# Three early tiles with additions on GpSimd, and the fourth quad's rows prepared sooner, in an embedding and CIN kernel

## The chip, the core and the metric

The kernel runs on one core of one Trainium2 chip. The metric is the device time of one execution, in microseconds. Three runs of the kernel before took 682.30, 683.49 and 684.36 us; their median is 683.49 us. The profiled execution took 684.21 us, and the span that its trace covers is 682.3 us.

## What is computed

512 samples have 39 features each. Every feature is looked up in its own table (16 floats a row), and three CIN layers of 128 maps, then a small MLP, follow:

```python
e = jnp.stack([tbl_0[ids[:, 0]], ..., tbl_38[ids[:, 38]]], axis=1)      # 512 x 39 x 16
def _cin_layer(X0, Xi, W, b):
    Wr = W.reshape(H, F0_, Fi)
    return jnp.einsum('hjk,bjd,bkd->bhd', Wr, X0, Xi) + b[None, :, None]
Xi = X0
for W, b in Ws:                     # three layers
    Xi = _cin_layer(X0, Xi, W, b)
    res.append(Xi.sum(axis=2))
h = jnp.concatenate([z, dense_ctx], axis=1)
h = jnp.maximum(h @ W_top1 + b_top1, 0.0)
h = jnp.maximum(h @ W_top2 + b_top2, 0.0)
y = h @ W_top3
```

Only the sum over the 16 positions of layers 2 and 3 is wanted, which the kernel uses.

## The kernel before

**Tiles and quads.** A tile is 8 samples by 16 positions, 128 partitions. There are 64 tiles, T = 0 to 63; four of them make a quad, q = 0 to 15. Tile T belongs to quad T // 4, and ti = T % 4 is its place there.

**A tile's work (layer 1 of the code).** TensorE makes ten groups of up to four features, g = 0 to 9 (group 8 has three). Each group is three matmuls (L995, L996, L997: a product of split numbers) into one of five PSUM banks, bank g % 5. Group g can begin only when the bank's last reader is through with group g - 5, or with group g + 5 of the tile before (L987). Groups 2, 5 and 8 are read by VectorE, which scales and adds up in `scale_and_sum` (L802); the other seven are read by ScalarE, which scales them into `prod` (`scale`, L611). So group 3 of a tile waits for VectorE's group 8 of the tile before. `y_made` counts the groups that TensorE has finished: 10 T + g + 1 behind group g of tile T.

**The reductions.** `reduce_early(T)` on VectorE (L809) sums what ScalarE's first five groups (0, 1, 3, 4, 6) left in `prod`, and stands on VectorE's queue between its groups 5 and 8. `reduce_late(T)` (L817) sums the rest and stands ahead of the next tile's group 2. From quad 2 on (FREE_QUADS = 2), GpSimd first adds four of the ten pairs of `prod` onto others, in two additions of a tile (`add_groups`, L428; the first waits for ScalarE's group 1, the second for its group 4), and the early reduction is over six pairs; it waits for GpSimd then. In tiles 0 to 7 GpSimd makes no additions, and the early reduction is over all ten. ScalarE's first group of the next tile waits for the early reduction (`scale`, L608).

**A quad's rows.** What layer 0 of quad q needs runs through every engine, ahead of its use:
1. GpSimd makes the indices and issues ten gathers, 0 to 9 (`gather`, L399). Those of quads 2 to 4 are gated by `GATHERED_AT`, a count of y_made for each.
2. SyncE waits for all ten to land and copies the rows to `emb_room` in 16 DMAs (`lay_out`, L297).
3. GpSimd repeats them in `emb_room` when these have landed (`repeat_rows`, L411 and L413).
4. TensorE turns them into `ps_tr` (`turn_rows`, L879), and ScalarE keeps the result as x0 (`keep_x0`, L535). For quads 1 and 2 this is done at the places in NEXT_TURNED_AFTER and NEXT_KEPT_AFTER, for quad 3 (during quad 1) at THIRD_TURNED_AFTER = (3, 1) and THIRD_KEPT_AFTER = (3, 3), which are a ti and a group of quad 1, and for later ones at TURNED_AFTER and KEPT_AFTER.
5. SyncE shares x0 out (`share_rows`, three DMAs, L305) and cuts six windows (`cut_window`, L310), and then lays out the next quad's rows.
6. GpSimd multiplies seven chunks (`multiply`, L423). Chunk 0 waits for the shared rows, chunk 1 for all six windows.
7. TensorE sums the seven chunks (`layer0`, L910), between the groups of the quad before. ScalarE and VectorE split the result (`keep_x1`, L546; `split_x1`, L727; `sum_x1`, L732).

**Order.** Every engine runs its own queue in the order written. GpSimd's for quads 0 and 1 is written out by hand (L466 to L500), and the loop over tiles with `between` (L502 to L520) begins with tile 8. TensorE's other work (`sum_d`, L1012, behind group 6; `turn_x`, L887; `turn_w2`, L900) stands between groups too.

Of the kernel before, what the change touches and what calls it, by code (L numbers as in the profile page):

```python
# [8 lines left out]
AX_XY = mybir.AxisListType.XY  # L9
# [11 lines left out]
QT = 4  # L21
# [9 lines left out]
GATHERS = -(-F // FPG)  # L31
# [23 lines left out]
ADDED = [(0, 1), (2, 3)]  # L55
EARLY = slice(4, 10)
EARLY_FIRST = slice(0, 10)
LATE = [slice(10, 16), slice(11, 17)]
ACCS = [10, 16]
BIASED = 15  # L60
# [12 lines left out]
REPEATED_IN = (1, 1)  # L73
TURNED_AFTER, KEPT_AFTER = (2, 4), (2, 6)
FREE_QUADS = 2
THIRD_TURNED_AFTER, THIRD_KEPT_AFTER = (3, 1), (3, 3)
SUMMED_AFTER = {(0, 2): 0, (0, 5): 1, (0, 8): 2, (1, 1): 3, (1, 8): 4, (2, 8): 5, (3, 2): 6}
THIRD_SUMMED_AFTER = {(0, 4): 0, (0, 7): 1, (0, 9): 2, (1, 2): 3, (1, 8): 4, (2, 8): 5, (3, 2): 6}
SECOND_SUMMED_AFTER = {(1, 9): 0, (2, 1): 1, (2, 3): 2, (2, 5): 3, (2, 7): 4, (3, 0): 5, (3, 2): 6}
# [3 lines left out]
SECOND_REGROUPED_AFTER = 3  # L83
NEXT_TURNED_AFTER, NEXT_KEPT_AFTER = [(0, 7), (0, 1)], [(0, 7), (0, 3)]

GATHERED_AT = {2: [0, 8, 9, 11, 13, 15, 17], 3: [0, 0, 0, 0, 42, 44, 46, 48, 50, 52],
               4: [54, 56, 58, 66, 68, 72, 73, 75, 76, 78]}
SUM_D_AFTER = 6

# [26 lines left out]
def wait(engine, semaphore, value):  # L116
    if value > 0:
        engine.wait_ge(semaphore, value)


def gather_rows(g):
# [3 lines left out]
def laid_through(q):  # L125

    return 16 * FPG * DG * (q - 1)


def chunk_rows(c):  # L130
    return F * sum(c + CHUNKS * a < SHIFTS for a in range(SPC))


def build(nc, dense_ctx, ids, bases, table, W_top1, b_top1, W_top2, b_top2, W_top3, W0, b0, W1, b1, W2, b2, out):
# [8 lines left out]
    with ExitStack() as ctx:  # L143
        def sb(name, shape, dt=F32):
            return ctx.enter_context(nc.sbuf_tensor(name, shape, dt))

        def sem(name):
            return ctx.enter_context(nc.semaphore(name))
# [40 lines left out]
        prod = sb("prod", [P, PAIRS, H, 2])  # L189
# [66 lines left out]
        dve_step, act_step, pool_step = sem("dve_step"), sem("act_step"), sem("pool_step")  # L256
# [32 lines left out]
        def _(sp):  # L289
            def lay_out(q):  # L290
                wait(sp, gathered[q % 2], 16 * GATHERS * (q // 2 + 1))
                wait(sp, emb_turned, q)
                for f in range(FPG):
                    n = len(range(f, F, FPG))
                    src = rows[QB * f:QB * (f + 1), q % 2, 0:n, :]
                    for e in range(DG):
                        sp.dma_start(packed[QB * e:QB * (e + 1), f:F:FPG, :],  # L297
                                     src[:, :, DI * e:DI * (e + 1)]).then_inc(laid_out, 16)

            def share_rows(q, landed):  # L300

                wait(sp, z_made, CHUNKS * q)
                for a in range(SPC):
                    at = -CHUNKS * a % F
                    sp.dma_start(xa[F * a:F * (a + 1), :], x0[at:at + F, q % 2, :]).then_inc(landed, 16)  # L305
# [77 lines left out]
        def _(pool):  # L383
            def make_index(q):

                wait(pool, laid_out, laid_through(q - 2) if q > 3 else 0)
                if q == 2:
                    pool.wait_ge(regrouped_dve, 1)
                    pool.wait_ge(regrouped_act, 1)
                if q == 3:  # L390
                    pool.wait_ge(regrouped_pool, 1)
                    pool.wait_ge(regrouped_act, 2)
                nc.gpsimd.tensor_tensor(index[:, q % 2, :], ids_all[:, q * GATHERS:(q + 1) * GATHERS], base[:],
                                        ALU.add).then_inc(index_made, 1)
                wait(pool, index_made, q + 1)

            def gather(q, g):
                n = gather_rows(g)
                pool.indirect_dma_start(  # L399
                    out=rows[0:n, q % 2, g, :], out_offset=None, in_=table,  # L400
                    in_offset=bass.IndirectOffsetOnAxis(ap=index[0:n, q % 2, g:g + 1], axis=0),
                ).then_inc(gathered[q % 2], 16)

            def repeat_rows(q):
                if q == 1:
                    pool.wait_ge(regrouped_pool, 1)
                    pool.wait_ge(regrouped_act, 2)
                else:
                    pool.wait_ge(laid_out, laid_through(q))
                n, last = F * DI, (XROWS - REP) * DI  # L410
                nc.gpsimd.tensor_copy(emb_room[:, n:SPC * n].rearrange("p (r n) -> p r n", n=n),  # L411
                                      emb_room[:, None, 0:n].broadcast_to([P, SPC - 1, n]))
                nc.gpsimd.tensor_copy(emb_room[:, SPC * n:SPC * n + last], emb_room[:, 0:last]).then_inc(emb_made, 1)  # L413

            def multiply(q, c):
                if c == 0:
                    wait(pool, shared[q % 2], 16 * SPC * ((q + 1) // 2))
                    wait(pool, z_used, CHUNKS * (q - 1) + 1)
                if c == 1:
                    wait(pool, cut[q % 2], 16 * (CHUNKS - 1) * ((q + 1) // 2))  # L420
                r = chunk_rows(c)
                window = bz[0:r, c, :] if c else x0[0:r, q % 2, :]
                nc.gpsimd.tensor_tensor(bz[0:r, c, :], window, xa[0:r, :], ALU.mult).then_inc(z_made, 1)  # L423
# [43 lines left out]
            def gather_behind(q, g):  # L467
                wait(pool, y_made, GATHERED_AT[q][g])
                gather(q, g)

            for g in range(len(GATHERED_AT[2])):
                gather_behind(2, g)
            for c in range(CHUNKS):
                multiply(1, c)
                if len(GATHERED_AT[2]) + c < GATHERS:
                    gather(2, len(GATHERED_AT[2]) + c)
            make_index(3)
            for g in range(4):
                gather_behind(3, g)
            repeat_rows(2)  # L480
            for g in range(4, 8):
                gather_behind(3, g)
            multiply(2, 0)
            for g in range(8, GATHERS):
                gather_behind(3, g)
            multiply(2, 1)
            multiply(2, 2)
            make_index(4)
            for g in range(3):
                gather_behind(4, g)  # L490
                multiply(2, 3 + g)
            multiply(2, 6)
            for g in range(3, 5):
                gather_behind(4, g)
            repeat_rows(3)
            for g in range(5, 9):
                gather_behind(4, g)
            multiply(3, 0)
            gather_behind(4, 9)
            multiply(3, 1)  # L500
# [169 lines left out]
        def _(dve):  # L670
# [82 lines left out]
            n, last = F * DI, (XROWS - REP) * DI  # L753
# [50 lines left out]

            def reduce_early(T):
                dve.wait_ge(act_step, ACT_STEPS * T + 5)
                wait(dve, pool_step, len(ADDED) * (T + 1 - FREE_QUADS * QT))
                wait(dve, reduced, REDUCTIONS * T)
                nc.vector.tensor_reduce(prod[:, BIASED, :, 0], prod[:, EARLY if T >= FREE_QUADS * QT else EARLY_FIRST].rearrange("p n h l -> p h n l"), AX_XY,  # L809
                                        ALU.add).then_inc(reduced, 1)  # L810

            def reduce_late(T):
# [11 lines left out]
            for T in range(TILES):  # L824
# [16 lines left out]
                if ti == 3 and FREE_QUADS <= q < QUADS - 1:  # L841
                    split_x1(q + 1)
                    sum_x1(q + 1)
                reduce_early(T)
                if T == 0:
                    split_rest_x1()
# [6 lines left out]
                if T in W2_TURNED_IN:  # L853
                    n = W2_TURNED_IN[T]
# [256 lines left out]
```

## Time and profile before

| | before |
|---|---|
| median of three runs | 683.49 us |
| profiled execution | 684.21 us |
| its span | 682.3 us |
| TensorE (PE) | 664.0 us busy, 97% |
| ScalarE (ACT) | 567.3 us busy, 83% |
| VectorE (DVE) | 512.4 us busy, 75% |
| GpSimd (POOL) | 443.4 us busy, 65% |

The profile is one execution taken by the hardware's profiler. "Busy" is the time in which an engine had at least one instruction under way. Matmuls are pipelined, so two records next to each other overlap by some 0.16 us, and the idle time in a row is a little less than what was lost. In a timeline a row is a start, a length, the engine, the line of the kernel, the operation with what it writes and reads, how many instructions were merged, and in brackets the idle time ahead of it with the engine and line that ended it. The releaser is inferred, and where a DMA or another wait came last it can name the wrong one.

### The profile page before, as it was taken

The numbers are of one execution on the slowest core, as the hardware profiler recorded it, in microseconds if no ns is written. First come the engines' busy times: TensorE is split into PE (matmuls) and PEld (weight loads), VectorE is DVE, ScalarE is ACT, GpSimd is POOL, SyncE is SP. The second block draws the span as 40 slices with busy tenths as digits, with TensorE's granted clock in tenths as the row PEclk, the third lists the DMA queues.
The fourth block names the chain that finished last, engine by engine and source line by source line (L and its number), as shares of the span: only waits on it lengthen the run. The fifth ranks groups of instructions, "written<-read, shape, count | busy, mean of one in ns | idle before, by whom it ended". The sixth has DMA issues, their size and how long they took to land.

```text
span 682.3 us, 10404 instructions
## 1 busy us (share of the span) xinstructions
PE 664.0 (97%) x2702; PEld 491.7 (72%) x2702; DVE 512.4 (75%) x984; ACT 567.3 (83%) x1997; POOL 443.4 (65%) x437
## 2 busy tenths in 40 slices
PE   4899999999999999999999999999999999999998
PEld 4766776677777777777777777777777777776683
DVE  5687887687787778777877787787878777888680
ACT  3586978798888888898988889888989898998672
POOL 6658374887778877788787777887788556333000
PEclk9899999999999999999999999999999999999899
DMA  6231234232423333333312212131313141005200
GB/s 211 77 96 9 56 58 120 38 98 11 153 40 110 85 94 99 68 98 68 97 8 77 29 38 65 13 90 5 98 7 98 5 139 37 0 1 184 116 1 1
DMA packets 107533, 46.04 MB, mean 67 GB/s; under 512 B 80897, under 2 KB 92941, under 8 KB 107474
## 3 DMA queue, kind: packets, MB, share of 16 engines
q1 hardware_dynamic: 101427, 42.82, 23.8%
q0 software_dynamic: 5120, 1.29, 2.2%
q10 hardware_dynamic: 927, 1.26, 0.7%
q8 instruction: 22, 0.36, 0.2%
q14 instruction: 37, 0.30, 0.1%
HBM read 13.81 MB, written 5.24 MB: 28 GB/s over the span
## 4 chain that ended last, share of the span: by engine, by line
PE 83%; ACT 1%; issue 1%; POOL 1%; DVE 0%; DMA 0%; SPq 0%; ACTq 0%; DVEq 0%; POOLq 0%
PE ps_y L995 19%; PE ps_y L997 18%; PE ps_y L996 18%; PE ps_x L910 12%; PE ps_g L1012 4%; PE ps_tr L879 1%; PE ps_y L1058 1%; PE ps_y L1056 1%; PE ps_y L1057 1%; ACT prod L611 1%; PE ps_y L1070 1%; PE ps_y L1006 1%; PE ps_tr L887 1%; PE ps_tr L900 1%; POOL room L423 1%
## 5 line engine op out<-in xcount | busy, mean ns | idle before, releaser
L611 ACT ACTIVATE prod<-ps_y,xt 128x128 f32<-128x128 f32 x1792 | 493.9, 431 | 75.2 <-PE ps_y L997 67.4
L995 PE MATMUL ps_y<-w_hi,x_hi 128*128 128x512 f32 (+1 forms) x640 | 312.8, 489 | 5.2 <-DVE prod L802 2.5
L996 PE MATMUL ps_y<-w_lo,x_hi 128*128 128x512 f32 (+1 forms) x640 | 249.6, 390 | 0.0
L997 PE MATMUL ps_y<-w_hi,x_lo 128*128 128x512 f32 (+1 forms) x640 | 249.5, 390 | 0.0
L428 POOL TENSOR_TENSOR prod<-prod 128x512 f32<-128x512 f32 x112 | 144.5, 1291 | 99.5 <-ACT prod L611 97.5
L802 DVE SCALAR_TENSOR_TENSOR prod<-ps_y,xt,prod 128x128 f32<-128x128 f32 x576 | 165.0, 344 | 45.1 <-PE ps_y L997 44.7
L399 POOL DMA_INDIRECT rows<-in_table,index x160 | 154.1, 963 | 49.6 <-issue 26.5
L809 DVE TENSOR_REDUCE prod<-prod 128x128 f32<-128x1536 f32 (+1 forms) x64 | 120.6, 1884 | 65.7 <-ACT prod L611 65.7
L995 PEld LDWEIGHTS ps_y<-w_hi,x_hi 128*128 128x128 f32 x640 | 120.8, 189 | 58.6 <-issue 24.6
L996 PEld LDWEIGHTS ps_y<-w_lo,x_hi 128*128 128x128 f32 x640 | 121.0, 189 | 48.5 <-issue 25.0
L423 POOL TENSOR_TENSOR room<-room 117x512 f32<-117x512 f32 (+1 forms) x105 | 135.2, 1290 | 24.2 <-DMA room<-room 21.4
L997 PEld LDWEIGHTS ps_y<-w_hi,x_lo 128*128 128x128 f32 x640 | 120.8, 189 | 25.9
L817 DVE TENSOR_REDUCE x<-prod 128x128 f32<-128x1536 f32 x64 | 112.0, 1750 | 13.2 <-ACT prod L611 10.9
L910 PE MATMUL ps_x<-room,w0t 117*128 117x512 f32 (+1 forms) x210 | 108.0, 595 | 1.5 <-POOL room L423 1.4
L910 PEld LDWEIGHTS ps_x<-room,w0t 117*128 117x128 f32 (+1 forms) x210 | 38.6, 189 | 9.3 <-POOL room L423 3.3
L1012 PE MATMUL ps_g<-bd,x 128*128 128x320 f32 x128 | 44.8, 431 | 0.0
L800 DVE TENSOR_SCALAR prod<-ps_y,xt 128x128 f32<-128x128 f32 x128 | 38.6, 344 | 0.4 <-PE ps_y L997 0.4
L620 ACT COPY g_all<-ps_g 128x320 f32<-128x320 f32 x64 | 31.2, 488 | 3.4 <-PE ps_g L1012 3.4
L655 ACT CAST g_hi<-g_all 128x512 fp32r<-128x512 f32 x39 | 23.9, 621 | 6.2 <-PE ps_y L1058 4.0
L1012 PEld LDWEIGHTS ps_g<-bd,x 128*128 128x128 f32 x128 | 24.0, 188 | 6.1 <-DVE x L817 0.5
L720 DVE TENSOR_TENSOR bd<-ps_tr,mask 128x1248 f32<-128x1248 f32 x16 | 23.2, 1448 | 0.0
L869 DVE TENSOR_TENSOR x_hi<-g_all,g_hi 128x512 fp32r<-128x512 f32 x20 | 13.8, 691 | 5.5 <-ACT g_hi L655 5.5
(120 smaller groups left out, 329.1 us busy)
## 6 DMA issues: line engine op xcount, KB each, us to landing
room<-room SPq DMA_DIRECT2D x75, 234.0 KB
room<-room SPq DMA_DIRECT2D x45, 78.0 KB
emb_room<-rows SPq DMA_DIRECT2D x168, 5.0 KB
rows<-in_table,index POOLq DMA_INDIRECT x160
w_hi_dram<-g_all SPq DMA_DIRECT2D x5, 512.0 KB, 4.3
w_lo_dram<-g_all SPq DMA_DIRECT2D x5, 512.0 KB, 5.1
room<-room SPq DMA_DIRECT2D x15, 156.0 KB
g_all<-in_L_rec_W SPq DMA_DIRECT2D x9, 256.0 KB, 6.0
```

Source lines behind the costliest of these rows:

```text
L399: pool.indirect_dma_start(out=rows[0:n, q % 2, g, :], out_offset=None, in_=table, in_offset=bass.IndirectOffsetOnAxis(ap=index[0:n, q % 2, ...
L423: nc.gpsimd.tensor_tensor(bz[0:r, c, :], window, xa[0:r, :], ALU.mult).then_inc(z_made, 1)
L428: nc.gpsimd.tensor_tensor(prod[:, SLOT[a]:SLOT[a] + 2], prod[:, SLOT[a]:SLOT[a] + 2], prod[:, SLOT[b]:SLOT[b] + 2], ALU.add).then_inc(pool ...
L611: ins = nc.scalar.activation(prod[:, SLOT[k] + m // 2, :, m % 2], ps_y[:, g % YBANKS, m * H:(m + 1) * H], ACT.Copy, scale=xt[:, q % 2, ti, ...
L802: ins = nc.vector.scalar_tensor_tensor(out=a, in0=y, scalar=x, in1=a, op0=ALU.mult, op1=ALU.add)
L809: nc.vector.tensor_reduce(prod[:, BIASED, :, 0], prod[:, EARLY if T >= FREE_QUADS * QT else EARLY_FIRST].rearrange("p n h l -> p h n l"), ...
L817: nc.vector.tensor_reduce(x2[:, T % 2, :], prod[:, LATE[T % 2]].rearrange("p n h l -> p h n l"), AX_XY, ALU.add).then_inc(reduced, 1)
L910: nc.tensor.matmul(ps_x1[:], w0t[0:r, c, :], bz[0:r, c, :], start=c == 0, stop=c == CHUNKS - 1).then_inc(z_used, 1)
L995: nc.tensor.matmul(y, hi, w1_hi[:, cols], start=True, stop=False)
L996: nc.tensor.matmul(y, hi, w1_lo[:, cols], start=False, stop=False)
L997: nc.tensor.matmul(y, lo, w1_hi[:, cols], start=False, stop=True).then_inc(y_made, 1)
L1012: nc.tensor.matmul(ps_g[:, 0:(F + 1) * TB], x2[:, T % 2, :], bd[:, T // QT % 2, T % QT].rearrange("p j b -> p (j b)"), start=True, stop=Tr ...
```

## The change

It touches tiles 0 to 7 only.

- GpSimd makes its two additions in tiles 3, 4 and 7 too, and VectorE's early reduction of these is over six pairs. The new function `adds(T)` tells which tiles have them, and the reduction's count of GpSimd's steps is made with it.
- The gates of quad 3's last six gathers go down by four groups each.
- On GpSimd's queue, the additions stand: tile 3's behind gather 3 of quad 3 and ahead of repeat_rows(2); tile 4's around gather 7 of quad 3; tile 7's around gather 7 of quad 4. Gather 8 of quad 3 moves ahead of multiply(2, 0), and repeat_rows(3) moves from behind gather 4 of quad 4 to behind multiply(2, 6), ahead of gather 3.
- TensorE turns quad 3's rows behind group 9 of tile 6 instead of behind group 1 of tile 7, and ScalarE keeps them behind its group 0 of tile 7 instead of its group 3.

```diff
-THIRD_TURNED_AFTER, THIRD_KEPT_AFTER = (3, 1), (3, 3)
+
+ADDED_EARLY = [3, 4, 7]
+THIRD_TURNED_AFTER, THIRD_KEPT_AFTER = (2, 9), (3, 0)
...
-GATHERED_AT = {2: [0, 8, 9, 11, 13, 15, 17], 3: [0, 0, 0, 0, 42, 44, 46, 48, 50, 52],
+GATHERED_AT = {2: [0, 8, 9, 11, 13, 15, 17], 3: [0, 0, 0, 0, 38, 40, 42, 44, 46, 48],
...
+def adds(T):
+    return T >= FREE_QUADS * QT or T in ADDED_EARLY
...
             make_index(3)
             for g in range(4):
                 gather_behind(3, g)
+            add_groups(3, 0)
+            add_groups(3, 1)
             repeat_rows(2)
-            for g in range(4, 8):
+            for g in range(4, 7):
                 gather_behind(3, g)
+            add_groups(4, 0)
+            gather_behind(3, 7)
+            add_groups(4, 1)
+            gather_behind(3, 8)
             multiply(2, 0)
-            for g in range(8, GATHERS):
-                gather_behind(3, g)
+            gather_behind(3, 9)
             multiply(2, 1)
             multiply(2, 2)
             make_index(4)
@@
                 gather_behind(4, g)
                 multiply(2, 3 + g)
             multiply(2, 6)
+            repeat_rows(3)
             for g in range(3, 5):
                 gather_behind(4, g)
-            repeat_rows(3)
-            for g in range(5, 9):
+            for g in range(5, 7):
                 gather_behind(4, g)
+            add_groups(7, 0)
+            gather_behind(4, 7)
+            add_groups(7, 1)
+            gather_behind(4, 8)
             multiply(3, 0)
             gather_behind(4, 9)
             multiply(3, 1)
...
             def reduce_early(T):
                 dve.wait_ge(act_step, ACT_STEPS * T + 5)
-                wait(dve, pool_step, len(ADDED) * (T + 1 - FREE_QUADS * QT))
+                if adds(T):
+                    dve.wait_ge(pool_step, len(ADDED) * sum(adds(t) for t in range(T + 1)))
                 wait(dve, reduced, REDUCTIONS * T)
-                nc.vector.tensor_reduce(prod[:, BIASED, :, 0], prod[:, EARLY if T >= FREE_QUADS * QT else EARLY_FIRST].rearrange("p n h l -> p h n l"), AX_XY,
+                nc.vector.tensor_reduce(prod[:, BIASED, :, 0], prod[:, EARLY if adds(T) else EARLY_FIRST].rearrange("p n h l -> p h n l"), AX_XY,
                                         ALU.add).then_inc(reduced, 1)
```

## Rows read from the trace of the kernel before

**Rows 1.** The page's first line.
```profile
span 682.3 us, 10404 instructions
```

**Rows 2.** TensorE's waits between 60 and 600 us: total, times, longest.
```profile
PE ps_y L995 <- DVE prod L802: 2.5, 2, 1.4
PE ps_x L910 <- POOL room L423: 0.7, 1, 0.7
```

**Rows 3.** TensorE's timeline, 75 to 129 us: start us, us, then what ran.
```profile
75.04 0.40 PE L997 MATMUL ps_y<-w_hi,x_lo 128*128 128x512 f32 x1
75.56 0.50 PE L995 MATMUL ps_y<-w_hi,x_hi 128*128 128x512 f32 x1
...
84.31 0.50 PE L995 MATMUL ps_y<-w_hi,x_hi 128*128 128x512 f32 x1 [1.13 <-DVE prod L802]
...
101.82 0.40 PE L995 MATMUL ps_y<-w_hi,x_hi 128*128 128x512 f32 x1
...
115.33 0.50 PE L995 MATMUL ps_y<-w_hi,x_hi 128*128 128x512 f32 x1 [1.39 <-DVE prod L802]
...
121.67 1.13 PE L910 MATMUL ps_x<-room,w0t 117*128 117x512 f32 x2 [0.74 <-POOL room L423]
...
123.64 0.40 PE L997 MATMUL ps_y<-w_hi,x_lo 128*128 128x512 f32 x1
124.15 1.12 PE L910 MATMUL ps_x<-room,w0t 117*128 117x512 f32 x2
...
127.22 1.02 PE L910 MATMUL ps_x<-room,w0t 117*128 117x512 f32 x2
128.28 0.49 PE L995 MATMUL ps_y<-w_hi,x_hi 128*128 128x512 f32 x1
```

**Rows 4.** VectorE's timeline: early reductions of tiles 3, 4, 7, 8; two others.
```profile
71.91 2.82 DVE L809 TENSOR_REDUCE prod<-prod 128x128 f32<-128x2560 f32 x1 [0.28 <-ACT prod L611]
...
80.66 2.82 DVE L809 TENSOR_REDUCE prod<-prod 128x128 f32<-128x2560 f32 x1 [0.83 <-ACT prod L611]
83.40 0.86 DVE L802 SCALAR_TENSOR_TENSOR prod<-ps_y,xt,prod 128x128 f32<-128x128 f32 x3
...
111.68 2.82 DVE L809 TENSOR_REDUCE prod<-prod 128x128 f32<-128x2560 f32 x1 [0.76 <-ACT prod L611]
...
125.69 1.75 DVE L809 TENSOR_REDUCE prod<-prod 128x128 f32<-128x1536 f32 x1 [5.53 <-ACT prod L611]
...
137.41 1.74 DVE L817 TENSOR_REDUCE x<-prod 128x128 f32<-128x1536 f32 x1
```

**Rows 5.** GpSimd's timeline, 71 to 139 us.
```profile
71.01 0.44 POOL L411 COPY emb_room<-emb_room 128x312 f32<-128x312 f32 x1 [3.85 <-DMA emb_room<-rows]
...
85.60 0.92 POOL L399 DMA_INDIRECT rows<-in_table,index  x1 [0.31 <-PE ps_y L997]
89.24 2.54 POOL L423 TENSOR_TENSOR room<-room 117x512 f32<-117x512 f32 x2 [2.72 <-PE ps_y L997]
...
98.18 2.53 POOL L423 TENSOR_TENSOR room<-room 117x512 f32<-117x512 f32 x2
...
120.34 1.27 POOL L423 TENSOR_TENSOR room<-room 117x512 f32<-117x512 f32 x1 [4.20 <-DMA room<-room]
...
138.61 1.29 POOL L428 TENSOR_TENSOR prod<-prod 128x512 f32<-128x512 f32 x1 [0.91 <-ACT prod L611]
```

**Rows 6.** ScalarE's timeline: tile 4's first groups, x0 of quads 2, 3.
```profile
74.82 3.26 ACT L611 ACTIVATE prod<-ps_y,xt 128x128 f32<-128x128 f32 x12 [0.54 <-issue]
77.88 0.66 ACT L535 COPY room<-ps_tr 123x512 f32<-123x512 f32 x1
...
108.96 0.61 ACT L535 COPY room<-ps_tr 123x512 f32<-123x512 f32 x1
```

**Rows 7.** SyncE's issues of lay_out for quads 2 and 3.
```profile
58.40 11.28 SPq L297 DMA_DIRECT2D emb_room<-rows  x16
...
89.43 10.60 SPq L297 DMA_DIRECT2D emb_room<-rows  x16
```

## Prediction

> **What bounds the kernel now.** I read the page's span and its busy shares first, then TensorE's waits, then TensorE's timeline, and only then the engines it waited for. The span is 682.3 us [rows 1] and TensorE is busy for 97% of it. Between 60 and 600 us it waits three times, 3.2 us in total: twice for VectorE's L802, once for GpSimd's L423 [rows 2]. All three lie before 122 us. From there on the kernel is as long as TensorE's own stream, so what happens on another engine counts only where it reaches TensorE before about 130 us.
>
> The waits view understates the loss, since the records of pipelined matmuls overlap. A group's L997 starts 0.23 us before the next matmul starts in an undisturbed stretch, and an L910 pair 0.46 us. Whatever is more is lost. Read so, the timeline [rows 3] has six losses from tile 4 on:
> - 0.29 us before 75.56 (tile 4, group 3: 75.56 - 75.04 - 0.23)
> - 1.30 us before 84.31 (tile 5, group 3: 1.13 idle, plus the 0.17 of overlap)
> - 1.55 us before 115.33 (tile 8, group 3: 1.39 + 0.16)
> - 0.90 us before 121.67 (layer 0 of quad 3, chunk 1: 0.74 + 0.16)
> - 0.28 us before 124.15 (chunk 2: 0.51 - 0.23)
> - 0.60 us before 128.28 (tile 9, group 3: 1.06 - 0.46)
>
> They add up to 4.92 us, which is the most that this change can win.
>
> Two causes stand behind them. Group 3 of a tile needs the PSUM bank of the tile before's group 8, which VectorE reads right after the early reduction. In quads 0 and 1 that reduction is over ten pairs and takes 2.82 us; with GpSimd's additions it takes 1.75 us [rows 4]. In tile 4 it starts at 80.66, group 8 follows at 83.40 and is done at 84.26, and TensorE goes on at 84.31. In tile 7 it starts at 111.68 and TensorE goes on at 115.33. Tile 3's does the same for the 0.29. The other three losses are quad 3's rows: its multiply of chunk 1 on GpSimd stood until 120.34 for the windows [rows 5], which came 10.8 us after x0 was kept (108.96 + 0.61 = 109.57) [rows 6]. Behind that multiply tile 8's additions were queued too, so its early reduction stood 5.53 us, to 125.69 [rows 4], and tile 9 lost its 0.60.
>
> **Part 1: additions in tiles 3, 4 and 7.** Six additions of 1.29 us are added on GpSimd [rows 5], 7.7 us; three reductions lose 2.82 - 1.75 = 1.07 us each on VectorE. An addition can end no sooner than ScalarE's group 4 plus 1.3 us, while the reduction waits for ScalarE's group 6 anyway, 1.0 us behind group 4 (a group of four is 3.26/12 x 4, about 1.0) [rows 6]. So the reduction starts about 0.3 us later than with ScalarE alone.
> - Tile 3: ScalarE's group 6 released the reduction at 71.91; its group 4 ended near 70.9, so the second addition runs to 72.2, and the reduction goes from 72.25 to 74.0 instead of to 74.73. Group 8 is done about 74.8: the 0.29 is gone. ScalarE had been idle 0.54 before 74.82, released by this reduction; it now starts tile 4 at 74.1, 0.7 sooner, and keeps quad 2's x0 at 77.2 instead of 77.88 [rows 6].
> - The additions stand ahead of quad 2's repeat_rows on GpSimd's queue, which ran at 71.01 when its copies had landed [rows 5]. It now ends near 72.7 instead of 71.6. Its reader, turn_rows(2), comes after tile 4's group 1, at 73.8: 1.1 us of cover, cost nothing.
> - Tile 4: ScalarE's groups 0 and 1 end by 76.25 and group 4 (behind the x0 copy) by 78.8. GpSimd: repeat_rows to 72.7; gathers 4, 5 and 6 of quad 3 to 76.3 (1.25 each, the last gated by tile 4's group 1); first addition 76.35 to 77.6; gather 7 to 78.7; second addition 78.85 to 80.1. Reduction 80.2 to 81.95, group 8 done at 82.8. TensorE wants group 3 of tile 5 at 84.31 - 1.30 - 0.29 = 82.7. So 0.1 is left of 1.30.
> - Tile 7: TensorE is then 1.5 us sooner (less the wait of part 2). ScalarE no longer copies x0 between groups 3 and 4 (0.47). The second addition ends near 110.2, the reduction runs 110.25 to 112.0, group 8 is done at 112.8, where TensorE wants it at 112.6: 0.25 is left of 1.55.
>
> The Trainium skill speaks against this part: "Perfetto Trace Analysis", section "Optimizing Scalar/DVE Operations", says that the two engines share an SBUF port, so that moving work from one to the other might not help. In this trace it does not show: an addition from 138.61 to 139.90 lies over a reduction from 137.41 to 139.15, and both have their usual lengths, 1.29 and 1.74 [rows 4, 5].
>
> **Part 2: quad 3 sooner.** The chain has four links, and each is set by a different engine.
> - Gathers. Their gates move four groups down, but the last one (9) is also behind multiply(2, 0), which waits for quad 2's x0 to be shared out. That comes 0.7 sooner (the copy above), at 82.2. The last gather therefore starts near 83.55 instead of 85.60 [rows 5]: 2.05 us won, not four groups.
> - Copies on SyncE. lay_out(3) started at 89.43, 3.83 after the last gather's start, and took 10.60 to issue [rows 7]. The copies of quad 2 were issued by 69.68 and GpSimd went on at 71.01, so they land 1.33 later. Now: 83.55 + 3.83 = 87.4, issued by 98.0, landed by 99.35. It is not delayed by SyncE's queue, whose window cuts for quad 2 end before 85.3.
> - repeat_rows(3) now stands right behind multiply(2, 6). That one ended at 100.71, 11.47 us after the windows of quad 2 came at 89.24 [rows 5]; the windows come 0.7 sooner, so it ends at 100.0. Then 0.59 for the repeat: 100.6. So GpSimd's own queue is later than the copies, by 0.6.
> - turn_rows(3) stands at the end of tile 6, where TensorE arrives at 101.82 - 1.5 = 100.3 [rows 3]. It waits about 0.3. This is a new wait, and behind it on TensorE's queue is all of tile 7. The turn itself (0.70) is only moved.
>
> What it brings: x0(3) is kept after tile 7's group 0, near 103.7 instead of 109.57. By the 10.8 us above chunk 1 has its windows at 114.4 instead of 120.34. GpSimd meets this after gathers, additions and multiply(3, 0) at 113.7; chunk 1 is multiplied by 115.7, chunk 2 by 118.2, tile 8's second addition ends at 119.7. TensorE wants chunk 1 at 118.3 and chunk 2 at 120.5 (before's times less the losses removed), and tile 9's group 3 at 124.0, for which group 8 is ready at 122.2. So 0.90, 0.28 and 0.60 all go, with 1.8 us or more of cover each.
> Quad 4's rows: their last gather is still behind multiply(3, 0), and goes from 115.2 to 112.7; its copies land by 129, ahead of GpSimd's repeat near 130.5. Cost nothing.
>
> **The sum.** 0.29 + 1.20 - 0.30 + 1.30 + 0.90 + 0.28 + 0.60 = 4.27 us, call it 4.25. Behind 130 us there was no wait to absorb or to renew it, and the end follows TensorE one to one. Span 682.3 - 4.25 = 678.05. The profiled execution took 684.21, so it would take 679.96; the three runs have the median 683.49, 0.72 below it, which gives **679.2 us**.
>
> **Rivals.**
> - *The turn waits longer.* Were the gathers' landing tied to the windows' traffic, so that lay_out(3) went no sooner than before (issued by 100.03), the rows would land at 101.4, be repeated at 102.0, and TensorE would wait 1.7 instead of 0.3: 4.25 - 1.4 gives 680.6. For it: 3.83 us for one gather's landing is long and falls in the cuts' traffic. Against: the windows are cut sooner as well. 12%.
> - *The additions come too late.* Gathers stand ahead of them with 0.1 us to spare in tile 4. One gather's slip (1.25) puts both second additions back; 1.1 of tile 5's and 1.2 of tile 8's losses return: gain 1.9, 681.6. Against: ScalarE's group 4, and not the queue, comes last by the times above. 12%.
> - *Quad 3's rows come sooner but the losses at 121 to 128 stay*, because GpSimd is late in tile 8 with one thing or another (six extra operations, 7.7 us). Gain 4.25 - 1.78 = 2.5, 681.0. Against: 2.6 us of cover on chunk 1. 8%.
> - *Port*: reductions and additions take turns. An addition then ends up to 1.75 later, so the losses of tiles 5 and 8 return in full (2.5): 681.7. The Trainium skill's page "SBUF — State Buffer", section "SBUF: two separate sides", calls the pair an exclusive lock for some operations. The overlapping rows speak against it. 3%.
> - *Slower.* TensorE stands at turn_rows(3) for more than it wins: the gain ahead of that wait and behind it is 4.55, so it decides once the rows are repeated later than 100.3 + 4.55 = 104.9. With copies 7 us later than worked out (107) it is 2 us slower, 685.5. Against it: before, GpSimd found the rows landed by 103.1. 3%.
>
> **How the numbers follow.** The forecast has 62%; its own range is 678.2 to 680.4 (a wait of 0 to 1.2 at the turn, 0.3 either way on each reduction, and the runs' scatter). The range for 8 in 10 goes from 677.9 (all 4.92, and a median 0.7 below) to 681.9, which takes in the rivals at 680.6, 681.0 and 681.6. Within 0.3%, about what a measurement of this kernel can tell from no change, means above 681.4: half of the late additions, the port and a part of the others, 16%. Slower by more: 4%. Faster by more: 80%.
>
> **What would show it.** TensorE's waits for L802 fall from 2.5 us to about 0.2 and the one for L423 is gone; there is a short new one at L879 near 100.5. Tile 4's early reduction takes 1.75 and starts near 80.2. The last gather of quad 3 starts near 83.5, lay_out(3) at 87.4, x0(3) is kept near 103.1. A wait at L879 of over 1 us, or additions that start long after ScalarE's group 4, would prove it wrong.

## Result and the profile after

The first comparison (six runs of each) gave the changed kernel a median of 677.94 us against 683.44, a ratio of 0.9922 with the 95% interval 0.991 to 0.9934. Two later comparisons of the same kernel (e1 and e11) gave 0.9946 (0.993 to 0.9963) and 0.9953 (0.9929 to 0.9976). They are not quite of one mind: by their medians the gain is 5.5, 3.9 and 3.6 us, by their ratios 5.3, 3.7 and 3.2. In the two profiles of the first comparison 2.9 us of the difference lie outside the work that was changed, as shown below. What the change itself brings is 3.6 to 3.7 us by the traces (three of the changed kernel against one of before).

The page after, first lines (share of the span, instructions). TensorE's share is 98% instead of 97%, over a span that is 6.6 us shorter [rows 1]:

```profile
span 675.7 us, 10410 instructions
PE 659.9 (98%) x2702; PEld 489.6 (72%) x2702; DVE 509.4 (75%) x984; ACT 568.2 (84%) x1997; POOL 452.4 (67%) x443
```

Line numbers have moved: L1011 to L1013 were L995 to L997, L817 was L802, L825 was L809, L833 was L817, L434 was L428, L429 was L423, L895 was L879, L1028 was L1012, L926 was L910, L626 was L611, L417 and L419 were L411 and L413. In e2's kernel these numbers are one higher from L550 on. TensorE's waits between 60 and 600 us, where before had 3.2 us [rows 2]:

```profile
PE ps_y L1011 <- DVE prod L817: 0.5, 2, 0.3
```

And its timeline at the four places that matter [rows 3]:

```profile
81.08 0.40 PE L1013 MATMUL ps_y<-w_hi,x_lo 128*128 128x512 f32 x1
81.68 0.50 PE L1011 MATMUL ps_y<-w_hi,x_hi 128*128 128x512 f32 x1 [0.20 <-DVE prod L817]
...
98.95 0.39 PE L1013 MATMUL ps_y<-w_hi,x_lo 128*128 128x512 f32 x1
99.41 1.16 PE L895 MATMUL ps_tr<-ident,emb_room 128*123 128x128 f32 x4
100.33 0.48 PE L1011 MATMUL ps_y<-w_hi,x_hi 128*128 128x512 f32 x1
...
111.35 0.40 PE L1013 MATMUL ps_y<-w_hi,x_lo 128*128 128x512 f32 x1
112.00 0.50 PE L1011 MATMUL ps_y<-w_hi,x_hi 128*128 128x512 f32 x1 [0.26 <-DVE prod L817]
...
117.44 1.02 PE L926 MATMUL ps_x<-room,w0t 117*128 117x512 f32 x2
```

Three small losses are left: 81.68 - 81.08 - 0.23 = 0.37 us at tile 5's group 3 (1.30 before), 0.42 at tile 8's (1.55 before), and at the turn 0.23 ahead of it plus 0.22 within it (99.41 to 100.33 is 0.92, where before's turn took 0.70). The losses at chunks 1 and 2, at tile 4's group 3 and at tile 9's are gone: the pair at 117.44 follows its neighbour at once.

**A ruler for the change.** Everything that was edited lies between TensorE's sum_d in tile 2 and the one in tile 9. Before, they start at 60.00 and 131.74, 71.74 us apart. After:

```profile
58.68 0.70 PE L1028 MATMUL ps_g<-bd,x 128*128 128x320 f32 x2
...
126.69 0.70 PE L1028 MATMUL ps_g<-bd,x 128*128 128x320 f32 x2
```

That is 68.01, so the stretch is **3.73 us** shorter. By losses it is 4.92 - 0.37 - 0.45 - 0.42 = 3.68: the two ways of reading agree in sum (e4 shows that single losses are less exact). The spans differ by 6.6: 1.3 us of that had come before tile 2, and 1.6 came behind 600 us, neither place touched. The windows of both profiles show what differed there. First before, then after (busy us and instructions of each engine; the column behind POOL is TensorE's mean granted clock as a share of the full one):

```profile
28.00:32.00 4.00, 4.00 (x12) 3.00 (x11) 2.27 (x6) 2.30 (x8) 1.62 (x2) 0.62 0.55 164
620.00:640.00 20.00, 20.00 (x60) 11.03 (x59) 13.03 (x24) 12.51 (x41) 2.60 (x2) 0.91 0.69 256
```

```profile
28.00:32.00 4.00, 4.00 (x17) 2.70 (x16) 1.89 (x5) 2.82 (x11) 1.84 (x3) 1.00 0.58 173
620.00:640.00 20.00, 20.00 (x69) 11.80 (x68) 14.76 (x23) 13.60 (x31) 1.30 (x1) 1.00 0.55 212
```

Before's profiled run had two stretches of lower clock, the changed kernel's had none.

### The profile page after: what moved, and what is told of

The parts are those of the page before. It is cut to its first block, busy times and chain, and to the rows that moved or that the text cites. A ratio compares the mean times of both kernels' runs of the same rounds, so it can differ in the third digit from the quotient of the medians.

```text
span 675.7 us, 10410 instructions
## 1 busy us (share of the span) xinstructions
PE 659.9 (98%) x2702; PEld 489.6 (72%) x2702; DVE 509.4 (75%) x984; ACT 568.2 (84%) x1997; POOL 452.4 (67%) x443
## 4 chain that ended last, share of the span: by engine, by line
PE 81%; ACT 1%; issue 0%; DVE 0%; POOL 0%; DVEq 0%; ACTq 0%
PE ps_y L1011 19%; PE ps_y L1013 18%; PE ps_y L1012 18%; PE ps_x L926 12%; PE ps_g L1028 4%; PE ps_tr L895 1%; PE ps_y L1074 1%; PE ps_y L1073 1%; PE ps_y L1072 1%; ACT prod L626 1%; PE ps_y L1086 1%; PE ps_y L1022 1%; PE ps_tr L903 1%; PE ps_tr L916 1%; PE ps_tr L1022 0%
## 5 line engine op out<-in xcount | busy, mean ns | idle before, releaser
L626 ACT ACTIVATE prod<-ps_y,xt 128x128 f32<-128x128 f32 x1792 | 494.9, 433 | 69.2 <-PE ps_y L1013 63.3
L1011 PE MATMUL ps_y<-w_hi,x_hi 128*128 128x512 f32 (+1 forms) x640 | 312.5, 488 | 3.3 <-issue 1.8
L1013 PE MATMUL ps_y<-w_hi,x_lo 128*128 128x512 f32 (+1 forms) x640 | 248.9, 389 | 0.0
L1012 PE MATMUL ps_y<-w_lo,x_hi 128*128 128x512 f32 (+1 forms) x640 | 248.8, 389 | 0.0
L434 POOL TENSOR_TENSOR prod<-prod 128x512 f32<-128x512 f32 x118 | 152.4, 1291 | 104.1 <-ACT prod L626 102.2
L817 DVE SCALAR_TENSOR_TENSOR prod<-ps_y,xt,prod 128x128 f32<-128x128 f32 x576 | 165.0, 343 | 45.4 <-PE ps_y L1013 45.1
L825 DVE TENSOR_REDUCE prod<-prod 128x128 f32<-128x1536 f32 (+1 forms) x64 | 117.4, 1834 | 63.1 <-ACT prod L626 63.1
L1011 PEld LDWEIGHTS ps_y<-w_hi,x_hi 128*128 128x128 f32 x640 | 120.5, 188 | 55.5 <-issue 24.6
L1012 PEld LDWEIGHTS ps_y<-w_lo,x_hi 128*128 128x128 f32 x640 | 120.7, 189 | 48.8 <-issue 25.2
L429 POOL TENSOR_TENSOR room<-room 117x512 f32<-117x512 f32 (+1 forms) x105 | 135.4, 1292 | 17.5 <-DMA room<-room 17.3
L1013 PEld LDWEIGHTS ps_y<-w_hi,x_lo 128*128 128x128 f32 x640 | 120.4, 188 | 25.7
L833 DVE TENSOR_REDUCE x<-prod 128x128 f32<-128x1536 f32 x64 | 112.0, 1749 | 12.9 <-ACT prod L626 10.5
L926 PE MATMUL ps_x<-room,w0t 117*128 117x512 f32 (+1 forms) x210 | 107.8, 594 | 0.5 <-POOL room L429 0.5
L1028 PE MATMUL ps_g<-bd,x 128*128 128x320 f32 x128 | 44.8, 431 | 0.0
L926 PEld LDWEIGHTS ps_x<-room,w0t 117*128 117x128 f32 (+1 forms) x210 | 38.8, 189 | 7.6 <-POOL room L429 1.4
L1028 PEld LDWEIGHTS ps_g<-bd,x 128*128 128x128 f32 x128 | 24.0, 188 | 6.1 <-DVE x L833 0.5
L895 PEld LDWEIGHTS ps_tr<-ident,emb_room 128*123 128x123 f32 x64 | 15.7, 311 | 1.8 <-issue 0.7
```

The source lines that it names most:

```text
L434: nc.gpsimd.tensor_tensor(prod[:, SLOT[a]:SLOT[a] + 2], prod[:, SLOT[a]:SLOT[a] + 2], prod[:, SLOT[b]:SLOT[b] + 2], ALU.add).then_inc(pool ...
L626: ins = nc.scalar.activation(prod[:, SLOT[k] + m // 2, :, m % 2], ps_y[:, g % YBANKS, m * H:(m + 1) * H], ACT.Copy, scale=xt[:, q % 2, ti, ...
L817: ins = nc.vector.scalar_tensor_tensor(out=a, in0=y, scalar=x, in1=a, op0=ALU.mult, op1=ALU.add)
L833: nc.vector.tensor_reduce(x2[:, T % 2, :], prod[:, LATE[T % 2]].rearrange("p n h l -> p h n l"), AX_XY, ALU.add).then_inc(reduced, 1)
L926: nc.tensor.matmul(ps_x1[:], w0t[0:r, c, :], bz[0:r, c, :], start=c == 0, stop=c == CHUNKS - 1).then_inc(z_used, 1)
L1011: nc.tensor.matmul(y, hi, w1_hi[:, cols], start=True, stop=False)
```

## Experiments

In each profile I read the same ruler, sum_d of tile 2 to sum_d of tile 9: 71.74 us before, 68.01 changed.

### e1: the changed kernel again

> The changed kernel again, beside the kernel before. TensorE's losses between 60 and 130 us add up to a gain of 3.7 us (4.92 lost before, 0.37 + 0.42 + 0.45 left), but the spans of the two profiles differ by 6.6 and the medians by 5.5. Theory 1 (the rest is scatter: a granted clock below 1.00 in stretches that the change does not touch, which fell on the profile of before): over five rounds the gain is 3.7 to 4.5 us, and both kernels show runs at 1.00 and below it. Theory 2 (the change itself moves the clock): the gain stays at 5.5, and the changed kernel's mean clock is above that of before in nearly every run.

Measured: 0.9946 (0.993 to 0.9963), 3.7 us. The ruler again read 68.01, but the span was 678.9, 3.2 us more than in the same kernel's first profile, and here the low clock is back in both places:

```profile
28.00:32.00 4.00, 4.00 (x12) 3.08 (x12) 1.95 (x5) 2.30 (x8) 1.94 (x2) 0.62 0.57 169
620.00:640.00 20.00, 20.00 (x61) 11.30 (x60) 13.12 (x25) 12.23 (x33) 2.34 (x2) 0.91 0.62 242
```

So theory 1: these dips come and go with the same instructions. The runs say it too. Over the comparisons of e1 to e8, before's runs with a mean clock of 1.000 have a mean of 681.3 us (11 runs), those at 0.997 682.4 (29) and those at 0.995 684.1 (11). The changed kernel's (its first comparison and e1) have 677.6 (5), 678.3 (8) and 680.8 (3). At equal clock the difference is 3.7, 4.1 and 3.3 us, and both kernels show the same three values. The runs of before are from two chips here, so this is a rough comparison.

### e2: the additions alone

```diff
-THIRD_TURNED_AFTER, THIRD_KEPT_AFTER = (2, 9), (3, 0)
+THIRD_TURNED_AFTER, THIRD_KEPT_AFTER = (3, 1), (3, 3)
-3: [0, 0, 0, 0, 38, 40, 42, 44, 46, 48]
+3: [0, 0, 0, 0, 42, 44, 46, 48, 50, 52]
```
(against the changed kernel; repeat_rows(3) is back behind gather 4 of quad 4, tile 4's additions stand around gather 6 of quad 3, and gather 8 is back behind multiply(2, 0).)

> Only the additions in tiles 3, 4 and 7; quad 3's rows as before. Theory 1 (the losses are in series: what tile 8 wins is waited for again at quad 3's chunk 1, since x0 of quad 3 is tied to tile 7's group 3): gain 1.2 us (0.29 + 0.93), tile 8's group 3 waits 0.4 and chunk 1 of quad 3 then about 2.0 instead of 0.90. Rival (the parts add): gain 2.35 us (1.2 and 1.13 at tile 8), chunk 1 waits 0.90 as before. If the clock theory 2 holds for the change as a whole, either may be 1 to 2 us more.

Measured: 1.0001 (0.9983 to 1.0019), the ruler 71.36, a gain of 0.38. TensorE at tile 8's group 3 and at chunks 1 and 2:

```profile
112.43 0.50 PE L1012 MATMUL ps_y<-w_hi,x_hi 128*128 128x512 f32 x1 [0.72 <-DVE prod L818]
...
119.58 1.12 PE L927 MATMUL ps_x<-room,w0t 117*128 117x512 f32 x2 [1.53 <-POOL room L429]
122.05 1.13 PE L927 MATMUL ps_x<-room,w0t 117*128 117x512 f32 x2
```

Tile 8's loss fell by 0.67 (1.55 to 0.88), and chunk 1's rose by 0.80 (0.90 to 1.70): in series, as the theory had it, and the gain of tile 8 is waited away. The gain had been put at 1.2, and two sizes were off. Tile 8 lost 0.88, not 0.4: ScalarE still copied x0 between tile 7's groups 3 and 4 (see e3). At tile 5 I had reckoned with 0.37 and 1.13 was lost. Gates 44 and 46 hold gathers 5 and 6, and the additions are queued behind them: the second one ran from 78.10 to 79.39, 19.8 us after sum_d of tile 2, against 19.0 (77.72 to 79.01) in the changed kernel. e6 asks the same more sharply.

### e3: quad 3's rows alone

```diff
-ADDED_EARLY = [3, 4, 7]
+ADDED_EARLY = []
```
(with the six add_groups calls taken out of GpSimd's queue.)

> Only quad 3's rows sooner (gathers, repeat, turn and keep), no additions in quads 0 and 1. Theory: the 0.90, 0.28 and 0.60 us at 121 to 128 us go, tiles 5 and 8 keep their 1.30 and 1.55; the rows are repeated near 101.0 and TensorE comes to the turn at 101.8, so it does not wait there. Gain 1.8 us. Rival (the rows are as late as before without tile 4's additions, which bring quad 2's x0 0.7 sooner): TensorE waits over 1 us at the turn and the gain is under 1 us.

Measured: 0.9966 (0.995 to 0.9983), 2.3 us; the ruler 69.57, a gain of 2.17. Chunk 1, chunk 2 and tile 9 lose nothing, tile 5 keeps 1.30, and TensorE does not wait at the turn. What I had not counted is tile 8: 1.08 instead of 1.55, since ScalarE no longer copies x0 between tile 7's groups 3 and 4 (0.47 us). With it, 0.90 + 0.28 + 0.60 + 0.47 = 2.25. The two halves give 0.4 and 2.2, together they give 3.7: the additions are worth 1.6 us once the rows are there and 0.4 before. Not all of that difference is a matter of losses in series. 0.80 us of it is chunk 1's longer wait in e2, but 0.76 is tile 5's (1.13 against 0.37), where e2's additions came later behind the old gates; the new wait at the turn (0.45) goes the other way.

### e4 and e5: the turn one group later

```diff
-THIRD_TURNED_AFTER, THIRD_KEPT_AFTER = (2, 9), (3, 0)
+THIRD_TURNED_AFTER, THIRD_KEPT_AFTER = (3, 0), (3, 1)
```
e5 has (3, 0), (3, 0).

> The changed kernel with quad 3's rows turned behind group 0 of tile 7 instead of group 9 of tile 6, and kept behind group 1. Theory: TensorE comes 0.7 us later and finds the rows, so its 0.45 us there is won, and the later x0 (1.2 us) is still in time for chunk 1: 0.4 us faster than the changed kernel. Rival (the wait only moves: x0 of quad 3 comes too late for chunk 1, or ScalarE is held up): no difference from the changed kernel.

> The changed kernel with quad 3's rows turned behind group 0 of tile 7 (instead of group 9 of tile 6), and kept behind group 0 as in the changed kernel. Measured from TensorE's sum_d in tile 2 to that in tile 9, before took 71.74 us, the changed kernel 68.01, the one with turn and keep both one group later 67.76: that one won the wait at the turn and lost 0.49 at tile 9's group 3, since chunk 1's windows came at 116.44. Theory: kept one group sooner, x0 comes 1 us sooner, tile 9 loses nothing and the stretch takes 67.3. Rival (ScalarE then stands for the turn and is late itself at tile 7): 67.8 or more.

Measured: e4 0.9942 (0.9925 to 0.996), e5 0.9928 (0.9908 to 0.9948), neither to be told from the changed kernel. The rulers read 67.76 and 67.87. In e4 the wait at the turn went, and TensorE started tile 9's group 3 late by 0.49: the windows came at 116.44 only, tile 8's additions stood behind that multiply, and the early reduction stood to 121.83. Chunk 1 itself was in time. What was thin was the cover of tile 9, 1.1 us in the changed kernel: x0 came 1.1 later and TensorE 0.45 sooner.

The losses of e4 do not add up to its ruler, though: 0.38 at tile 5, 0.43 at tile 8 and 0.49 here would make 68.1. The rows behind the start show why. First before, then the changed kernel, then e4, at tile 9's group 3:

```profile
128.28 0.49 PE L995 MATMUL ps_y<-w_hi,x_hi 128*128 128x512 f32 x1
128.61 0.39 PE L996 MATMUL ps_y<-w_lo,x_hi 128*128 128x512 f32 x1
```

```profile
122.48 1.02 PE L926 MATMUL ps_x<-room,w0t 117*128 117x512 f32 x2
122.94 0.79 PE L1011 MATMUL ps_y<-w_hi,x_hi 128*128 128x512 f32 x1
123.57 0.39 PE L1012 MATMUL ps_y<-w_lo,x_hi 128*128 128x512 f32 x1
```

```profile
123.46 1.02 PE L926 MATMUL ps_x<-room,w0t 117*128 117x512 f32 x2
124.41 0.50 PE L1011 MATMUL ps_y<-w_hi,x_hi 128*128 128x512 f32 x1
124.74 0.40 PE L1012 MATMUL ps_y<-w_lo,x_hi 128*128 128x512 f32 x1
```

Behind a pair of layer 0, the first matmul of a group takes 0.63 us to the next start where TensorE did not wait, and 0.33 where it did. So 0.30 of a wait at this place costs nothing: from the pair to the group's second matmul it is 1.09 us in the changed kernel, 1.28 in e4 and 1.39 before (127.22 to 128.61). Tile 9's loss was 0.30 and not 0.60, and e4's is 0.19 and not 0.49. At the other places a start behind a wait costs some 0.10 more than was counted (112.00 to the next start is 0.34, not 0.23). Both corrections together leave the gain by losses at 3.68. They bring e4 to 67.8, and the losses agree with the ruler within 0.1 us in every run but e6, whose clock dipped. So 0.45 was won in e4 and 0.19 given back.

e5's forecast of 67.3 had taken off the whole 0.49; with 0.19 it would have been 67.6. In e5 the loss at tile 9 is gone, and TensorE waited at the turn all the same. That wait, and not ScalarE as the rival had it, is the rest. The rows in e5:

```profile
98.46 0.40 PE L1013 MATMUL ps_y<-w_hi,x_lo 128*128 128x512 f32 x1
98.79 1.16 PE L895 MATMUL ps_tr<-ident,emb_room 128*123 128x128 f32 x4
99.79 1.02 PE L926 MATMUL ps_x<-room,w0t 117*128 117x512 f32 x2
```

Its rows were repeated by 98.74, 41.2 us after sum_d of tile 2, against 40.7 in the changed kernel and 40.6 in e4. Its GpSimd had stood until 86.77 for the windows, 29.3 after the same point against 28.7. The start is 0.10 late and the turn takes 0.22 longer than in e4, 0.3 together. The landing of DMAs differed by half a microsecond between these executions, as much as the term in question.

### e6: the old gates

```diff
-3: [0, 0, 0, 0, 38, 40, 42, 44, 46, 48]
+3: [0, 0, 0, 0, 42, 44, 46, 48, 50, 52]
```

> The changed kernel with the gates of quad 3's gathers as before (42 to 52 instead of 38 to 48), the order of GpSimd's queue as changed. Theory (the lower gates matter less for the gathers themselves than for the additions queued behind them): tile 4's second addition comes some 1.8 us later, tile 5's group 3 loses about 2.1 us instead of 0.37, the wait at the turn goes (TensorE comes later), and the stretch from tile 2's sum_d to tile 9's takes 69.3 us (68.01 in the changed kernel). Rival (the gates serve only to bring the rows sooner): tile 5 loses 0.4, the wait at the turn grows, 69.0 by the turn alone.

Measured: 0.9964 (0.9945 to 0.9984), the ruler 71.23, where 69.3 was expected. Tile 5's group 3 lost 2.55 us (2.1 expected), and the wait at the turn went. GpSimd's additions of tile 4, and TensorE behind them:

```profile
77.81 1.30 POOL L434 TENSOR_TENSOR prod<-prod 128x512 f32<-128x512 f32 x1
80.25 1.30 POOL L434 TENSOR_TENSOR prod<-prod 128x512 f32<-128x512 f32 x1
```

```profile
84.22 0.50 PE L1011 MATMUL ps_y<-w_hi,x_hi 128*128 128x512 f32 x1 [2.38 <-DVE prod L817]
84.56 0.40 PE L1012 MATMUL ps_y<-w_lo,x_hi 128*128 128x512 f32 x1
...
85.16 0.63 PE L1011 MATMUL ps_y<-w_hi,x_hi 128*128 128x512 f32 x1
85.58 0.63 PE L1012 MATMUL ps_y<-w_lo,x_hi 128*128 128x512 f32 x1
```

71.74 - 4.92 + 2.55 + 0.42 is 69.8; the other 1.4 us are matmuls that start 0.42 apart instead of 0.23, in a stretch of 4 us where the mean granted clock was 0.61. The timed runs gain 2.4 us by their ratio, where this profile's stretch gains 0.5, so most of them will not have had that dip there, which is not shown. The low clock followed TensorE's wait of 2.4 us here. It did not in e7's profile, after a wait of 3.0, so this is one case and not a rule. The gates' worth lies in the queue: the additions stand behind them, and so does multiply(2, 0) with gather 9 behind it. The rows came later too. The last gather started 25.1 us after sum_d of tile 2, against 23.55 in the changed kernel, and GpSimd stood for the copies before it repeated them, 2.3 us later than in the changed kernel:

```profile
101.42 0.44 POOL L417 COPY emb_room<-emb_room 128x312 f32<-128x312 f32 x1 [1.59 <-DMA emb_room<-rows]
```

That cost nothing at the turn only because TensorE itself came there 3.7 us later, after its loss at tile 5 and the low clock. Without the low clock it would have come about when the rows did (an estimate: 44.2 - 1.4 = 42.8 us after sum_d of tile 2, against 42.95).

### e7: rows repeated behind two more gathers

```diff
-            repeat_rows(3)
             for g in range(3, 5):
                 gather_behind(4, g)
+            repeat_rows(3)
```

> The changed kernel with repeat_rows(3) behind gathers 3 and 4 of quad 4 on GpSimd's queue, as before the change. Two gathers are 2.5 us. Theory (TensorE's wait at the turn goes into the total one to one): the loss at the turn is 0.45 + 2.5 - about 0.1 = 2.8 to 3.0 us, the stretch from tile 2's sum_d to tile 9's takes 70.4 us, and the run is about 2.4 us slower than the changed kernel. Rival (the wait is hidden, since tile 7 and 8 are held by VectorE and by chunk 1 anyway): the losses at tile 8's group 3 shrink by as much as the turn's grow, and the stretch stays under 68.8.

Measured: 0.9994 (0.9977 to 1.0011), the ruler 70.91 (70.4 expected), 2.9 us more than the changed kernel:

```profile
98.75 0.39 PE L1013 MATMUL ps_y<-w_hi,x_lo 128*128 128x512 f32 x1
102.15 1.16 PE L895 MATMUL ps_tr<-ident,emb_room 128*123 128x128 f32 x4 [3.00 <-POOL emb_room L419]
```

The loss at the turn is 3.17 + 0.22 = 3.4 us, 2.9 more than the changed kernel's, and all of it is in the ruler, while tile 8's loss stayed at 0.42. This is the mechanism of the prediction's rival "Slower", brought about by the edit: a microsecond at that wait is a microsecond of the kernel, and two gathers in the wrong place take back most of the change.

### e8: no additions in tile 3

```diff
-ADDED_EARLY = [3, 4, 7]
+ADDED_EARLY = [4, 7]
```
(with tile 3's two calls taken out.)

> The changed kernel without tile 3's two additions (its early reduction over ten pairs again). Theory: tile 4's group 3 loses its 0.29 again, ScalarE starts tile 4 0.7 us later, so tile 5's group 3 loses about 0.8 instead of 0.37, and quad 2's x0 and all that hangs on it comes 0.7 later with TensorE: the stretch takes 68.7 us. Rival (tile 3's additions serve only tile 4's group 3): 68.3 us.

Measured: 0.9954 (0.9936 to 0.9971), the ruler 68.77 (68.7 expected). Tile 4's group 3 loses 0.29 and tile 5's 0.63 instead of 0.37. Tile 3's additions are worth 0.76 us, more than the 0.29 that they remove on the spot. By losses it is 0.39 at tile 4 (with the start behind a wait, see e4), 0.26 at tile 5 and 0.09 at the turn.

### e9, e10 and e11: the repeat ahead of the last chunk

```diff
-            multiply(2, 6)
             repeat_rows(3)
+            multiply(2, 6)
```
e10 also turns behind (3, 0); e11 is the changed kernel, in the same comparison.

> The changed kernel with repeat_rows(3) ahead of multiply(2, 6) instead of behind it. The prediction says that GpSimd's own queue, and not the copies' landing, sets the turn. Theory: in the changed kernel the copies were issued by 96.89 and landed near 98.2, GpSimd was through with chunk 5 at 97.55; so the rows are repeated by 98.8 instead of 99.35, TensorE comes at 99.2, the 0.45 us at the turn goes, and the stretch from tile 2's sum_d to tile 9's takes 67.6 us (68.01 in the changed kernel). Rival (the copies land later than that, so that they and not GpSimd set the turn): GpSimd stands for them in front of the repeat, the wait stays, 68.0.

> The same with quad 3's rows turned behind group 0 of tile 7, as in e5. Theory: no wait at the turn whatever the landing's scatter of some 0.5 us, 67.55 us for the stretch, 4.2 us faster than before and 0.4 faster than the changed kernel, which five rounds can hardly tell. Rival (as in e5, something else comes late by as much): 67.9 or more.

> The changed kernel once more, on the same chip as these two and for one more sample of it: 3.7 us faster than before by the stretch in its trace (68.01). If the 5.5 us of its first comparison were true and the 3.7 of e1 scatter, this one lies nearer to 5.5.

Measured: e9 0.9922 (0.9891 to 0.9952), e10 0.9958 (0.9933 to 0.9984), e11 0.9953 (0.9929 to 0.9976). All runs on this chip, before's too (median 690.6), were 7 to 9 us longer. In the three profiles the mean granted clock between 20 and 36 us was 0.69 to 0.71 (1.00 in the changed kernel's first one). The rulers read 68.06, 67.57 and 68.19. In e9 GpSimd stood in front of the repeat:

```profile
104.90 0.44 POOL L417 COPY emb_room<-emb_room 128x312 f32<-128x312 f32 x1 [0.96 <-DMA emb_room<-rows]
```

The copies had been issued by 103.56, so they landed 1.34 later, as the prediction had it. The rows were repeated at 105.48, just ahead of TensorE, which started the turn at 105.56 without a gap; the turn took 0.90 all the same, so 0.2 was lost instead of 0.45. But tile 5 lost 0.63 in this execution instead of 0.37, in work that was not edited against e11, and the ruler shows no gain. e10 has no wait at the turn (0.78 us from the first transpose to what follows, as in e4) and reads what was forecast, 67.57. In e11 GpSimd itself stood 0.29 us for the copies: the two things that set the turn, its queue and the landing, are within half a microsecond of each other, and either can be last. Neither e9 nor e10 is shown to be faster than the changed kernel by its timed runs.

## Why the prediction came out as it did

The forecast was 679.2 us with a gain of 4.25. The first comparison measured 677.94 and 5.5, inside the range by 0.04 us only; the later ones give gains of 3.9 and 3.6 by their medians.

- **The bound and the six losses: right in their places.** Nothing outside them changed in the stretch: 3.68 by losses, 3.73 by the ruler. "The most that this change can win" was put at 4.92. With the corrections of e4 it was 5.1: tile 9's loss was 0.30 and not 0.60, and each of the other five was some 0.10 larger. That the errors nearly cancel in the gain is luck. The 6.6 us between the spans do not contradict the ceiling, since 2.9 of them lie in stretches that the change does not touch; e1 has the same instructions with 3.2 us more.
- **Tile 4's additions: right in mechanism, 0.27 us too good.** The reduction started at 79.10, 20.42 after sum_d of tile 2, where the forecast (80.2 against 60.00) had 20.2: ScalarE's group 4 ended 0.2 later than I put it. So 0.37 was left instead of 0.1.

```profile
77.72 1.29 POOL L434 TENSOR_TENSOR prod<-prod 128x512 f32<-128x512 f32 x1 [0.16 <-ACT prod L626]
```

```profile
79.10 1.75 DVE L825 TENSOR_REDUCE prod<-prod 128x128 f32<-128x1536 f32 x1 [1.24 <-ACT prod L626]
```

- **Tile 7's: the same**, 0.42 left instead of 0.25. A part of this term was not the additions' at all: e3 shows that 0.47 of the 1.55 goes with ScalarE's copy of x0.
- **Tile 3's: right**, its 0.29, and ScalarE keeps quad 2's x0 0.63 us sooner (0.7 forecast); e8 gives both their price, 0.76.
- **The last gather comes 2 us sooner, not four groups: right.** It started 23.55 us after sum_d of tile 2 (82.23), forecast 23.55. lay_out(3) began 3.68 later (3.83 forecast) and took 10.98 (10.60).
- **The new wait at the turn: right in place, 0.15 too small.** The arrival came 40.5 us after sum_d of tile 2 and the repeat's end 40.7 (40.3 and 40.6 forecast), so the wait ahead of the turn was 0.23 (0.3 forecast). What I did not know is that a turn that had to wait takes 0.92 instead of 0.70 from its first transpose to what follows.

```profile
98.76 0.45 POOL L417 COPY emb_room<-emb_room 128x312 f32<-128x312 f32 x1
99.15 0.20 POOL L419 COPY emb_room<-emb_room 128x24 f32<-128x24 f32 x1
```

- **Chunks 1 and 2 and tile 9: right, all of these losses went** (put at 1.78, 1.7 with the corrections). Chunk 1 was multiplied by 115.16 for a TensorE that came at 117.44: 2.3 us of cover (2.6 forecast). Tile 9 had the least, 1.1 instead of 1.8, which is why e4 lost there.
- **The rivals.** The late turn is real and costs one to one (e7), but did not come. Late additions did not come either; e6 shows that it needs only the old gates. That the losses at 121 to 128 stay was wrong, that the reductions and additions take turns too: five early reductions and 59 shorter ones kept 2.82 and 1.75, and an addition lies over a late reduction (75.16 to 76.46 over 74.05 to 75.79) with both at their usual length.

```profile
75.16 1.30 POOL L434 TENSOR_TENSOR prod<-prod 128x512 f32<-128x512 f32 x1
```

```profile
74.05 1.74 DVE L833 TENSOR_REDUCE x<-prod 128x128 f32<-128x1536 f32 x1
```

In sum the stretch won 3.7 where 4.27 was forecast: 0.27 + 0.17 + 0.15 too little. That the first median nevertheless fell 1.3 us below the forecast is luck and no merit of the model: three comparisons of one kernel gave 5.5, 3.9 and 3.6.

What stays open: why the clock is granted lower in these stretches of some executions (28 to 32 and 620 to 640 us) and not in others. No run here varies its cause.

## What to carry to other kernels

- Where one engine is busy 97% of the time, list its losses one by one, from the distance between starts and not from idle time alone. Their sum is the ceiling, and each part of a change should be entered against one of them. Look one instruction past the wait, too: at tile 9 half of the apparent loss was given back there.
- Losses in series on one chain do not add. An early win is waited away at the next thing that is tied to a fixed time: the additions alone gave 0.4 us, the rows alone 2.2, both 3.7 (part of that gap was e2's later additions).
- On a hand-written queue a gate delays all that stands behind it. Read a gate's price from the last thing queued behind it (e6: 2.2 us more at tile 5, and rows 2.3 us later, from four groups on the gathers), and use a ruler between two marks around the edit when the whole execution scatters by more than the effect.

## What the runs showed of the hardware

- Four transposes that TensorE had to wait for took 0.92 us to the next start (changed kernel, e1, e7, e11), the same four without a wait 0.70 (before, e2, e3, e6). Ahead of layer 0's matmuls it was 1.00 with a wait (e5) and 0.78 without (e4, e10). In e9 the rows came 0.08 us ahead of the first transpose, and it was 0.90 without a gap ahead of them.
- Behind a pair of layer 0, a group's first matmul took 0.63 us to the next start without a wait and 0.33 with one (changed kernel; before and e4).
- The same instructions ran with a mean granted clock of 0.62 or 1.00 in the stretch of 28 to 32 us, and 0.91 or 1.00 at 620 to 640, from one execution to the next: 3.2 us of 677.
- SBUF-to-SBUF copies of lay_out were seen to have landed 1.33 to 1.34 us after the last one was issued (before, e3, e6, e9, e11). Quad 3's six windows came 10.7 to 11.2 us after x0 was kept, in eleven traces. The landing of quad 2's windows, counted from sum_d of tile 2, moved by 0.6 us between two executions (28.7 in the changed kernel, 29.3 in e5).
